# A two-block transformer kernel: attention of the second half before the router, the router on four banks, no filling products

## The chip, the cores and the metric

The kernel runs on one core of a Trainium2 chip. The metric is the device time of one launch in microseconds. A core has TensorE (PE, matrix products), VectorE (DVE), ScalarE (ACT), GpSimd (POOL) and SyncE (SP, which here only issues transfers). Each engine takes its instructions strictly in the order in which they are written; between engines, semaphores tell when a result is there. PSUM, where PE writes, has eight banks of 128 x 512 floats.

## The reference

Eight batches of 128 tokens, 512 wide, go through two blocks:

```
x += tanh(g_xattn[0]) * attention_32_heads(layernorm(x), ctx, rotary, mask)
x += tanh(g_ffn[0])   * (layernorm(x) @ dequantized(W).T + bias)
x += tanh(g_xattn[1]) * softmax(Q K^T / sqrt(512)) @ ctx        # Q from layernorm(x), K from ctx
xf = layernorm(x)                                               # 1024 tokens
logits = xf @ gate_w.T                                          # 32 experts
w, idx = top_k(logits, 2); w = softmax(w)
x += tanh(g_ffn[1]) * sum_k w[k] * (xf @ expert_w[idx[k]].T + expert_b[idx[k]])
```

## The kernel before

A "tile" is 128 tokens, one batch. Tiles 0 to 3 are the first half, 4 to 7 the second. The first attention and the feed-forward take up to about 700 us; the change touches what lies between there and the start of the experts.

**The second attention.** PE makes the query and key projections (`project(i)`, 12 products of 128x512 each), ACT moves each out of PSUM (`keep(i)`). `score(n)` makes the scores of half n into bank 4. DVE takes the maximum (`softmax_shift`), ACT the exponentials (`exps(n)`), PE transposes them into bank 5 (`turn_probs(n)`), ACT copies them (`probs_kept(n)`), PE multiplies with the context, one batch after another, on banks 6 and 7 (`attend(n, batches)`), and DVE adds the result to x and takes the statistics of the next norm (`attended(t)`). `attend` of a tile waits until DVE has emptied the same bank two tiles earlier.

**The router.** For each tile: ACT takes the root (`router_std`), DVE the reciprocal and the shift (`normed`), ACT writes the normalized tile (`router_norm`), PE transposes it (`router_turn`), ACT copies the transpose (`router_kept`), PE multiplies it with the gate weights, four products of 128x32 listed as eight (`logits`), DVE finds the two best experts (`choose`), POOL writes the 0/1 rows (`code`), PE counts how many tokens chose each expert before this one (`rank`), DVE picks the place (`find_place`), POOL marks it (`mark_place`), and PE lays the token numbers at their places (`codes`). Transposes and logits of tile t use bank t % 2, so `router_turn(t)` waits for the choice of tile t-2. `count_all` closes it, DVE reads the places (`write_rows`, place_row, line 1372) and POOL gathers the tokens of each expert by indirect transfers (`take(k)`, line 1048), which also need all eight normalized tiles written to memory (`keep_rows`, on SP).

**Filling products.** `fill(n)` on PE makes n products of 96x128 with 128x512 into bank 4 (line 1621). Nobody reads them. There are 58, between the router's steps and 18 behind `count_all`.

**The experts.** 36 slots follow. For slot k PE transposes the gathered tokens (`turn`, one slot ahead) and makes 12 products of 128x512 (`multiply`, lines 133 to 135). ACT and DVE split tokens and weights into an upper and a lower part. SP keeps a ring of nine expert weights of 1 MB each full; entries 2 to 6 are loaded once `score(1)` is done.

The order is written out by hand for every engine. Each engine's list stands at the end of its function.

Of the kernel before, what the change touches and what calls it, by code (L numbers as in the profile page):

```python
# [9 lines left out]
ALU = mybir.AluOpType  # L10
ACT = mybir.ActivationFunctionType
AX = mybir.AxisListType

P = 128
NB = 8
# [3 lines left out]
KC = E // P  # L19
# [21 lines left out]
def program(nc, a, out):  # L41

    root = ExitStack()
    with root:
# [764 lines left out]
        COMB = 2  # L809
        words = sb("words", [P, 2, KC, E], I32)  # L810
# [108 lines left out]

        def bank_of(k):  # L920
            return psum[(6, 7, 4, 2)[k % LANES]][:, :]
# [14 lines left out]
        with nc.Block() as block:  # L936
            @block.sync
            def _(sp):
# [20 lines left out]
                keep_rows(HALVES[0])  # L959
# [3 lines left out]
                keep_rows(HALVES[1])  # L963
# [38 lines left out]
            def _(pool):  # L1002
# [65 lines left out]
                for t in range(NB - 2):  # L1068
                    mark_place(t)
                    code(t + 2)  # L1070
                mark_place(NB - 2)
# [21 lines left out]
            def _(act):  # L1093
# [26 lines left out]
                def router_std(t):  # L1120
                    act.wait_ge(ln_aggr, 3 * NB + t + 1)
                    nc.scalar.activation(spread[:, t:t + 1], meanvar[:, t, 1:2], ACT.Sqrt, bias=eps[:, :]).then_inc(ln_std, 1)

                def router_norm(t):
                    act.wait_ge(ln_var, 6 + t + 1)
                    nc.scalar.activation(last_xn[:, t, :], x[:, t, :], ACT.Identity, scale=rstd[:, t:t + 1], bias=shift[:, t:t + 1]).then_inc(ln_norm, 1)

                def router_kept(t):
                    act.wait_ge(r_turned, t + 1)
                    after(act, r_logits, t - 1)  # L1130
                    nc.scalar.activation(xr[:, t % 2, :, :], psum[t % 2][:, :].rearrange("p (c t) -> p c t", c=KC), ACT.Copy).then_inc(r_kept, 1)
# [70 lines left out]
                router_std(0)  # L1202
                router_std(1)
                router_norm(0)
                keep(15)
                router_std(2)
                router_norm(1)
                router_std(3)
                router_norm(2)
                router_norm(3)  # L1210
# [5 lines left out]
                router_kept(0)  # L1216
                router_kept(1)
                exps(1)
                probs_kept(1)
                router_kept(2)  # L1220
                router_kept(3)
                router_std(4)
                router_std(5)
                router_norm(4)
                router_kept(4)
                router_std(6)
                router_norm(5)
                router_kept(5)
                router_std(7)
                router_norm(6)  # L1230
                router_kept(6)
                router_norm(7)
# [18 lines left out]
            def _(dve):  # L1251
# [65 lines left out]
                def normed(t):  # L1317
                    dve.wait_ge(ln_std, 6 + t + 1)
                    nc.vector.reciprocal(rstd[:, t:t + 1], spread[:, t:t + 1]).then_inc(ln_rstd, 1)
                    dve.wait_ge(ln_rstd, 6 + t + 1)  # L1320
                    nc.vector.scalar_tensor_tensor(shift[:, t:t + 1], meanvar[:, t, 0:1], -1.0, rstd[:, t:t + 1], ALU.mult, ALU.mult).then_inc(ln_var, 1)

                def choose(t):

                    scores = psum[t % 2][:, 0:NX]
# [130 lines left out]
                attended(1)  # L1456
                normed(0)
                attended(2)
                normed(1)
                attended(3)  # L1460
                normed(2)
                normed(3)
                softmax_shift(1)
                choose(0)
                choose(1)
                softmax_scale(1)
                find_place(0)
                attended(4)
                attended(5)
                normed(4)  # L1470
                choose(2)
                attended(6)
                normed(5)
                find_place(1)
                choose(3)
                attended(7)
                normed(6)
                choose(4)
                find_place(2)
                normed(7)  # L1480
                choose(5)
                find_place(3)
                choose(6)
                find_place(4)
                choose(7)
                find_place(5)
                find_place(6)
                find_place(7)
# [38 lines left out]
            def _(pe):  # L1527
# [55 lines left out]
                def router_turn(t):  # L1583
                    pe.wait_ge(ln_norm, 3 * NB + t + 1)
                    if t < 2:
                        pe.wait_ge(ln_lo, 3 * NB)
                    else:
                        pe.wait_ge(r_best, 2 * t - 2)
                    for c in range(KC):
                        mm = nc.tensor.transpose(psum[t % 2][:, c * P:(c + 1) * P], last_xn[:, t, c * P:(c + 1) * P], ident[:, :])  # L1590
                    mm.then_inc(r_turned, 1)

                def logits(t):
                    pe.wait_ge(g_gate, 16)
                    pe.wait_ge(r_kept, t + 1)
                    for c in range(KC):
                        mm = nc.tensor.matmul(psum[t % 2][:, 0:NX], xr[:, t % 2, c, :], gw[:, c, :], start=c == 0, stop=c == KC - 1)  # L1597
                    mm.then_inc(r_logits, 1)
# [18 lines left out]

                def fill(n):

                    for _ in range(n):  # L1620
                        nc.tensor.matmul(psum[4][:, :], ones[0:3 * NX, :], eb3[:, :], start=True, stop=True)  # L1621
# [96 lines left out]
                attend(0, range(4))  # L1718
                project(15)
                score(1)  # L1720
                for t in range(2):
                    router_turn(t)
                    logits(t)
                router_turn(2)
                router_turn(3)
                turn_probs(1)
                rank(0)
                attend(1, range(2))
                logits(2)
                logits(3)  # L1730
                rank(1)
                codes(0)
                attend(1, range(2, 4))
                pe.wait_ge(constants, 2)
                fill(4)
                router_turn(4)
                fill(4)
                logits(4)
                rank(2)
                codes(1)  # L1740
                fill(4)
                router_turn(5)
                fill(4)
                logits(5)
                rank(3)
                codes(2)
                fill(4)
                router_turn(6)
                fill(4)
                logits(6)  # L1750
                rank(4)
                fill(4)
                router_turn(7)
                codes(3)
                fill(4)
                logits(7)
                rank(5)
                codes(4)
                fill(4)
                rank(6)  # L1760
                codes(5)
                fill(2)
                rank(7)
                codes(6)
                fill(2)
                codes(7)
                count_all()
                fill(18)
# [75 lines left out]
```

## Time and profile before

| | us |
|---|---|
| median of 3 timed runs | 932.43 (931.3 to 934.28) |
| the profiled execution's own time | 926.58 |
| its span, first to last instruction | 924.8 |
| PE busy, of the span | 845.8 (91%) |
| DVE busy | 661.4 (72%) |
| ACT busy | 398.5 (43%) |
| mean granted clock of PE | 0.964 |

Times in rows are from the span's start. "Granted clock" is the share of PE's full speed of 2.4 GHz; 0.50 is 1.2 GHz. A busy PE isn't a PE that does needed work: the filling products count as busy.

### The profile page before, as it was taken

The numbers are of one execution on the slowest core, as the hardware profiler recorded it, in microseconds if no ns is written. First come the engines' busy times: TensorE is split into PE (matmuls) and PEld (weight loads), VectorE is DVE, ScalarE is ACT, GpSimd is POOL, SyncE is SP. The second block draws the span as 40 slices with busy tenths as digits, with TensorE's granted clock in tenths as the row PEclk, the third lists the DMA queues.
The fourth block names the chain that finished last, engine by engine and source line by source line (L and its number), as shares of the span: only waits on it lengthen the run. The fifth ranks groups of instructions, "written<-read, shape, count | busy, mean of one in ns | idle before, by whom it ended". The sixth has DMA issues, their size and how long they took to land. (4 is left out here: it accounts for less than half of the span.)

```text
span 924.8 us, 13194 instructions
## 1 busy us (share of the span) xinstructions
PE 845.8 (91%) x4370; PEld 708.1 (77%) x4370; DVE 661.4 (72%) x1311; ACT 398.5 (43%) x1012; POOL 431.2 (47%) x390
## 2 busy tenths in 40 slices
PE   5688999999999999999999999987989898989990
PEld 4676788888888888888888888866877676877870
DVE  4947688876778776788886788775372556999974
ACT  4334334424325433434433433444124545978970
POOL 5449636534626642734833633512020148876730
PEclk9878999999999999999999999999999998999995
DMA  8301301200200300110200120006100645999817
GB/s 330 152 1 46 114 1 35 80 1 2 84 31 0 113 0 0 45 68 1 84 29 0 45 91 1 1 1 245 46 11 1 232 178 193 340 351 337 331 43 274
DMA packets 23641, 91.13 MB, mean 99 GB/s; under 512 B 6576, under 2 KB 7088, under 8 KB 15776
## 3 DMA queue, kind: packets, MB, share of 16 engines
q1 hardware_dynamic: 17440, 81.00, 23.8%
q0 software_dynamic: 6144, 9.46, 2.9%
q8 instruction: 25, 0.41, 0.2%
q14 instruction: 32, 0.26, 0.1%
HBM read 86.23 MB, written 14.68 MB: 109 GB/s over the span
## 5 line engine op out<-in xcount | busy, mean ns | idle before, releaser
L359 POOL TENSOR_TENSOR qT<-straight,turned 128x512 f32<-128x512 f32 x64 | 82.5, 1290 | 154.8 <-DVE turned L557 154.5
L455 ACT ACTIVATE probs<-bank,negmax 128x128 f32<-128x128 f32 x256 | 90.5, 365 | 134.0 <-DVE negmax L568 134.0
L557 DVE TENSOR_TENSOR turned<-bank,sinT 64x512 f32<-64x512 f32 x160 | 110.1, 688 | 2.2
L133 PE MATMUL bank<-wo_hi,oT_hi 128*128 128x512 f32 x256 | 101.5, 397 | 8.2 <-DVE oT_lo L581 6.2
L133 PE MATMUL bank<-xT_hi,wq_hi 128*128 128x512 f32 x256 | 105.3, 411 | 1.0 <-POOL wq_lo L338 1.0
L135 PE MATMUL bank<-xT_hi,wq_lo 128*128 128x512 f32 x256 | 100.9, 394 | 0.0
L134 PE MATMUL bank<-xT_lo,wq_hi 128*128 128x512 f32 x256 | 100.7, 393 | 0.0
L135 PE MATMUL bank<-wo_hi,oT_lo 128*128 128x512 f32 x256 | 100.4, 392 | 0.0
L134 PE MATMUL bank<-wo_lo,oT_hi 128*128 128x512 f32 x256 | 100.3, 392 | 0.0
L462 ACT ACTIVATE pT_hi<-bank 128x512 fp32r<-128x512 f32 x64 | 38.3, 599 | 131.2 <-PE bank L722 131.2
L555 DVE TENSOR_TENSOR straight<-bank,cosT 128x512 f32<-128x512 f32 x80 | 55.2, 691 | 45.4 <-PE bank L135 44.9
L363 POOL TENSOR_TENSOR probs<-probs,invtotal 128x512 f32<-128x512 f32 x64 | 66.7, 1043 | 20.6 <-DVE invtotal L573 20.6
L1443 DVE TENSOR_TENSOR cT_lo<-ring,cT_hi 128x1024 fp32r<-128x1024 f32 x56 | 68.3, 1221 | 11.1 <-ACT cT_hi L1155 11.1
L715 PE MATMUL bank<-kT,qT 128*128 128x128 f32 x512 | 69.9, 281 | 5.8 <-POOL qT L359 5.8
L586 DVE SCALAR_TENSOR_TENSOR x<-bank,gates,x 128x512 f32<-128x512 f32 x64 | 47.9, 748 | 34.7 <-PE bank L135 34.7
L564 DVE COPY_PREDICATED_SCALAR bank<-closed_key,masked 128x128 f32 x256 | 71.1, 346 | 1.9 <-issue 1.8
L467 ACT ACTIVATE oT_hi<-bank 128x512 fp32r<-128x512 f32 x64 | 38.6, 604 | 73.7 <-PE bank L135 73.7
L715 PEld LDWEIGHTS bank<-kT,qT 128*128 128x128 f32 x512 | 63.9, 196 | 6.7 <-issue 4.6
L133 PE MATMUL bank<-cT_hi,xT_hi 128*128 128x512 f32 x144 | 60.5, 420 | 5.8 <-DVE xT_lo L1437 5.8
L133 PEld LDWEIGHTS bank<-wo_hi,oT_hi 128*128 128x128 f32 x256 | 48.3, 189 | 20.6 <-DVE oT_lo L581 7.5
L581 DVE TENSOR_TENSOR oT_lo<-bank,oT_hi 128x512 fp32r<-128x512 f32 x64 | 44.2, 691 | 25.0 <-ACT oT_hi L467 23.6
L1056 POOL DMA_INDIRECT picked<-loaded,place_row x36 | 44.2, 1227 | 33.6 <-ACT loaded L1161 25.2
(226 smaller groups left out, 2121.5 us busy)
## 6 DMA issues: line engine op xcount, KB each, us to landing
ring<-in_ew SPq DMA_DIRECT2D x28, 1024.0 KB, 8.3
raw_big<-in_wq SPq DMA_DIRECT2D x8, 1024.0 KB, 4.8
raw_big<-in_wo SPq DMA_DIRECT2D x8, 1024.0 KB, 4.8
early_w<-in_ew SPq DMA_DIRECT2D x8, 1024.0 KB, 8.0
ring<-picked SPq DMA_DIRECT2D x8, 512.0 KB, 6.9
raw_k<-in_wk SPq DMA_DIRECT2D x8, 256.0 KB, 5.0
ctx_raw<-in_ctxT SPq DMA_DIRECT2D x4, 512.0 KB, 6.1
raw_v<-in_wv SPq DMA_DIRECT2D x8, 256.0 KB, 5.0
```

Of the source, the lines that this page charges most:

```text
L133: nc.tensor.matmul(out_, hi, r_hi, start=start, stop=False)
L134: nc.tensor.matmul(out_, hi, r_lo, start=False, stop=False)
L135: return nc.tensor.matmul(out_, lo, r_hi, start=False, stop=stop)
L359: nc.gpsimd.tensor_tensor(dst, straight[:, k, :], turned[:, k, :], ALU.add).then_inc(rope_sum, 1)
L363: nc.gpsimd.tensor_tensor(probs[:, u % 2, :, :], probs[:, u % 2, :, :], invtotal[:, u % UNITS, :].unsqueeze(2).broadcast_to([P, GR, S]), A ...
L455: ex = nc.scalar.activation(probs[:, u % 2, h, :], bank_scores[u % 2][:, h * S:(h + 1) * S], ACT.Exp, bias=negmax[:, u % UNITS, h:h + 1], ...
L555: nc.vector.tensor_tensor(straight[:, k, :], bank[:, :], cosT[:, tok], ALU.mult)
L557: last = nc.vector.tensor_tensor(turned[dst, k, :], bank[src, :], sinT[src, tok], ALU.mult)
L564: kept_ = nc.vector.copy_predicated(bank_scores[u % 2][:, h * S:(h + 1) * S], closed_key[:, u, :], masked[:, :].broadcast_to([P, S]))
L586: nc.vector.scalar_tensor_tensor(x[:, u % UNITS, :], bank_y[:, :], gates[:, 0:1], x[:, u % UNITS, :], ALU.mult, ALU.add).then_inc(y_added, 1)
L715: mm = nc.tensor.matmul(bank_scores[u % 2][:, h * S:(h + 1) * S], qT[:, u // 4, h, q], kT[:, keys], start=True, stop=True)
L1443: nc.vector.tensor_tensor(expert_lo(k)[:, rows, :], ring[k % RING][:, rows, :], expert_hi(k)[:, rows, :].bitcast(F32), ALU.subtract).then_ ...
```

## The change

1. PE: `project(15)` stands ahead of the attention of the first half, `score(1)` behind two of its batches. The second half's probabilities and all four of its batches come before any router step. Then the router runs with nothing else between its steps.
2. All `fill` calls are gone.
3. The router has four banks, 0, 1, 4 and 5: `router_turn(t)` waits for the choice of tile t-4.
4. Root, reciprocal and shift are made for tiles 0-3, 4-5 and 6-7 together (`NORMED`), in 3 instructions of each kind for 8.
5. ACT: the exponentials of the second half come before the first root. DVE's order follows PE's.
6. SP: loads of ring entries 2 to 6 stand ahead of all writes of normalized tiles.
7. The marks of tiles 5, 6 and 7 are made by DVE, where only that of tile 7 was; POOL marks tiles 0 to 4.

```diff
+        MARKED = 5
+        NORMED = ((0, 4), (4, 6), (6, 8))
+        def router_bank(t):
+            return psum[(0, 1, 4, 5)[t % 4]]
...
-                keep_rows(HALVES[0])
                 sp.wait_ge(g_smm, 2)
                 for k in range(EARLY, RING - 2):
                     sp.dma_start(ring[k], a["ew"][k]).then_inc(w_in[k], 16)
-                keep_rows(HALVES[1])
+                keep_rows(TILES)
...
-                def router_std(t):
-                    act.wait_ge(ln_aggr, 3 * NB + t + 1)
-                    nc.scalar.activation(spread[:, t:t + 1], meanvar[:, t, 1:2], ACT.Sqrt, bias=eps[:, :]).then_inc(ln_std, 1)
+                def router_std(g):
+                    first, last = NORMED[g]
+                    act.wait_ge(ln_aggr, 3 * NB + last)
+                    nc.scalar.activation(spread[:, first:last], meanvar[:, first:last, 1], ACT.Sqrt, bias=eps[:, :]).then_inc(ln_std, 1)
...
-                    if t == NB - 1:
+                    if t >= MARKED:
                         dve.wait_ge(r_place, 2 * t + 2)
-                        dve.wait_ge(r_at, NB - 1)
+                        dve.wait_ge(r_at, t)
...
                 def router_turn(t):
                     pe.wait_ge(ln_norm, 3 * NB + t + 1)
-                    if t < 2:
+                    if t < 4:
                         pe.wait_ge(ln_lo, 3 * NB)
+                        pe.wait_ge(g_pkept, 2)
                     else:
-                        pe.wait_ge(r_best, 2 * t - 2)
+                        pe.wait_ge(r_best, 2 * t - 6)
...
+                for t in range(2, NB):
                     logits(t)
+                    if t + 2 < NB:
+                        router_turn(t + 2)
+                    rank(t - 1)
+                    codes(t - 2)
+                pe.wait_ge(g_added, NB)
...
-                fill(18)
                 turn(0)
```

PE's queue before, from the first half's attention to the router's fifth tile. `gw` are logits, `ident,words` transposes of router tiles, `l1_ctx` attention, `l1_k` scores, `eb3` filling products; the 12 products of a projection are left out.

```order
L1581 MATMUL bank7<-l1_ctx,l1_pT 128x512
...
L1563 MATMUL bank4<-l1_k,weight 128x128 x16
L1590 MATMUL bank0<-ident,words 128x128 x4
L1597 MATMUL bank0<-gw,x_router_4171 128x32 x4
...
L1581 MATMUL bank7<-l1_ctx,l1_pT 128x512
L1621 MATMUL bank4<-eb3_4190,ones_4168 128x512 x4
L1590 MATMUL bank0<-ident,words 128x128 x4
L1621 MATMUL bank4<-eb3_4190,ones_4168 128x512 x4
L1597 MATMUL bank0<-gw,x_router_4171 128x32 x4
L1607 MATMUL bank2<-chosen_4166,ones_4168 128x224
```

The same place in the changed kernel, with the same names (`l1_probs` is the transpose of the probabilities):

```order
L1570 MATMUL bank7<-l1_ctx,l1_pT 128x512
L1552 MATMUL bank4<-l1_k,weight 128x128 x16
L1570 MATMUL bank6<-l1_ctx,l1_pT 128x512
L1570 MATMUL bank7<-l1_ctx,l1_pT 128x512
L1560 MATMUL bank5<-ident,l1_probs 128x128 x4
...
L1570 MATMUL bank7<-l1_ctx,l1_pT 128x512
L1580 MATMUL bank0<-ident,words 128x128 x4
L1580 MATMUL bank1<-ident,words 128x128 x4
L1587 MATMUL bank0<-gw,x_router_4171 128x32 x4
L1580 MATMUL bank4<-ident,words 128x128 x4
```

The scores now come between two pairs of batches, and the first router transpose comes behind the last batch instead of behind the scores. Farther on, the changed queue repeats this for each tile, with nothing between (here the logits of tile 4, the transpose of tile 6, the count of tile 3 and the codes of tile 2):

```order
L1587 MATMUL bank0<-gw,x_router_4171 128x32 x4
L1580 MATMUL bank4<-ident,words 128x128 x4
L1597 MATMUL bank2<-chosen_4166,ones_4168 128x192
L1600 MATMUL bank2<-chosen_4166,before_4167 128x32
L1612 MATMUL bank3<-onehot_code_4169,xT_lo 128x32 x2
```

Before, eight filling products (line 1621) stood among these rows for every tile.

## Rows read from the trace of the kernel before

**Rows 1.** Busy time by stretch: PE, weight loads, DVE, ACT, POOL, clock, DMA share, GB/s.

```profile
727.60:768.18 40.58, 36.89 (x200) 29.95 (x198) 22.44 (x96) 16.43 (x31) 17.49 (x36) 0.87 0.59 220
768.18:925.00 156.82, 124.51 (x609) 100.69 (x607) 127.85 (x159) 107.70 (x150) 90.53 (x75) 0.92 0.76 274
```

**Rows 2.** Chain of waits, attention to first experts: start, us, what.

```profile
715.73 0.88 PE bank L1581 x2
...
723.80 3.84 PE bank L1563 x32
...
732.20 1.77 PE bank L1590 x8
...
746.71 0.93 PE bank L1621 x4
747.64 0.90 PE bank L1597 x8
748.97 1.01 PE bank L1621 x4
749.98 0.44 PE bank L1590 x4
...
770.95 4.11 DMA words<-xn_rows,place_token
775.11 0.66 PE bank L1656 x4
```

**Rows 3.** Busy time by stretches of 2 us, columns as in rows 1.

```profile
728.00:730.00 2.00, 1.22 (x12) 1.18 (x12) 0.61 (x3) 0.60 (x1) 0.56 (x1) 1.00 1.02 304
732.00:734.00 2.00, 2.00 (x11) 1.52 (x11) 0.84 (x5) 1.81 (x9) 0.50 (x2) 0.53 0.98 410
736.00:738.00 2.00, 2.00 (x10) 1.07 (x8) 1.12 (x2) 1.89 (x3) 0.92 (x2) 1.00 0.98 414
758.00:760.00 2.00, 1.08 (x6) 0.90 (x6) 0.44 (x2) 0.00 (x0) 1.97 (x5) 0.86 0.67 279
760.00:762.00 2.00, 1.97 (x8) 1.78 (x8) 0.55 (x3) 1.15 (x2) 0.00 (x0) 0.50 0.04 12
766.00:768.00 2.00, 2.00 (x10) 1.65 (x9) 1.44 (x3) 0.00 (x0) 1.84 (x3) 0.94 0.19 51
776.00:778.00 2.00, 2.00 (x7) 1.56 (x7) 1.38 (x3) 1.34 (x2) 1.59 (x2) 0.62 0.97 387
```

**Rows 4.** Costliest group of 714 to 768 us: busy, mean ns, idle before.

```profile
L1621 PE MATMUL bank<-eb,ones 96*128 96x512 f32 x58 | 19.1, 465 | 0.0
```

**Rows 5.** Timeline, instructions in order of time: start, us, engine, line [idle before].

```profile
727.67 2.77 SPq L962 DMA_DIRECT2D ring<-in_ew  x5
727.68 0.69 DVE L1295 TENSOR_REDUCE l_max<-bank 128x4 f32<-128x512 f32 x1 [2.47 <-PE bank L1563]
...
731.03 1.28 ACT L1112 ACT_TABLE_LOAD   x1
732.32 0.37 ACT L1112 ACTIVATE l_probs<-bank,l_nb 128x128 f32<-128x128 f32 x1
...
733.88 1.11 PE L1571 MATMUL bank<-ident,l_probs 128*128 128x128 f32 x4
...
742.38 0.60 PE L1590 MATMUL bank<-ident,words 128*128 128x128 f32 x4
...
743.02 0.60 ACT L1131 ACTIVATE x_router<-bank 128x512 f32<-128x512 f32 x1 [1.81 <-PE bank L1590]
...
743.70 0.80 ACT L1126 ACTIVATE words<-x,shift,rstd 128x512 f32<-128x512 f32 x1
...
743.76 1.05 PE L1597 MATMUL bank<-gw,x_router 128*128 128x32 f32 x8
...
761.96 0.19 DVE L1372 TENSOR_SCALAR place_row<-bank 128x32 int32<-128x32 f32 x1 [1.37 <-PE bank L1627]
761.97 6.37 PE L1621 MATMUL bank<-eb,ones 96*128 96x512 f32 x18
```

More of the change, by code:

```diff
@@ L1067, in _ @@
                 code(1)
-                for t in range(NB - 2):
+                for t in range(MARKED):
                     mark_place(t)
                     code(t + 2)
-                mark_place(NB - 2)
+                code(MARKED + 2)
                 pool.wait_ge(rows_out, 16 * NB)
@@ L1130, in router_kept @@
                     after(act, r_logits, t - 1)
-                    nc.scalar.activation(xr[:, t % 2, :, :], psum[t % 2][:, :].rearrange("p (c t) -> p c t", c=KC), ACT.Copy).then_inc(r_kept, 1)
+                    nc.scalar.activation(xr[:, t % 2, :, :], router_bank(t)[:, :].rearrange("p (c t) -> p c t", c=KC), ACT.Copy).then_inc(r_kept, 1)
                 def weight_exp():
@@ L1201, in _ @@
                 keep(14)
-                router_std(0)
-                router_std(1)
-                router_norm(0)
                 keep(15)
[L1206 to L1210, printed above, removed]
                 act.wait_ge(m_const, 64)
@@ L1215, in _ @@
                 nc.scalar.activation(eb3[:, :], eb_raw[:, :], ACT.Copy).then_inc(exact, 1)
-                router_kept(0)
-                router_kept(1)
                 exps(1)
                 probs_kept(1)
+                router_std(0)
+                router_norm(0)
+                router_norm(1)
+                router_kept(0)
+                router_std(1)
+                router_norm(2)
+                router_kept(1)
+                router_norm(3)
                 router_kept(2)
+                router_norm(4)
                 router_kept(3)
-                router_std(4)
-                router_std(5)
-                router_norm(4)
+                router_std(2)
+                router_norm(5)
                 router_kept(4)
-                router_std(6)
-                router_norm(5)
+                router_norm(6)
                 router_kept(5)
-                router_std(7)
-                router_norm(6)
+                router_norm(7)
                 router_kept(6)
-                router_norm(7)
                 router_kept(7)
@@ L1315, in attended, with normed @@
                     nc.vector.bn_aggr(meanvar[:, t, :], stats[:, t, :]).then_inc(ln_aggr, 1)
[L1317 to L1321, printed above, removed]
+                def normed(g):
+                    tiles = slice(*NORMED[g])
+                    dve.wait_ge(ln_std, 6 + g + 1)
+                    nc.vector.reciprocal(rstd[:, tiles], spread[:, tiles]).then_inc(ln_rstd, 1)
+                    dve.wait_ge(ln_rstd, 6 + g + 1)
+                    nc.vector.scalar_tensor_tensor(shift[:, tiles], meanvar[:, tiles, 0], -1.0, rstd[:, tiles], ALU.mult, ALU.mult).then_inc(ln_var, 1)
                 def choose(t):
-                    scores = psum[t % 2][:, 0:NX]
+                    scores = router_bank(t)[:, 0:NX]
                     dve.wait_ge(r_logits, t + 1)
@@ L1456, in _ @@
                 attended(1)
+                softmax_shift(1)
+                attended(2)
+                attended(3)
+                softmax_scale(1)
+                attended(4)
                 normed(0)
-                attended(2)
+                attended(5)
+                attended(6)
+                choose(0)
                 normed(1)
-                attended(3)
+                choose(1)
+                find_place(0)
+                attended(7)
+                choose(2)
                 normed(2)
[L1462 to L1473, printed above, removed]
-                find_place(1)
[L1475 to L1488, printed above, removed]
+                find_place(1)
+                for t in range(3, NB):
+                    choose(t)
+                    find_place(t - 1)
+                find_place(NB - 1)
                 weight_diff()
@@ L1596, in logits @@
                     for c in range(KC):
-                        mm = nc.tensor.matmul(psum[t % 2][:, 0:NX], xr[:, t % 2, c, :], gw[:, c, :], start=c == 0, stop=c == KC - 1)
+                        mm = nc.tensor.matmul(router_bank(t)[:, 0:NX], xr[:, t % 2, c, :], gw[:, c, :], start=c == 0, stop=c == KC - 1)
                     mm.then_inc(r_logits, 1)
@@ L1616, in count_all @@
                                      start=False, stop=True, skip_group_check=True).then_inc(r_rank, 1)
-                def fill(n):
-                    for _ in range(n):
-                        nc.tensor.matmul(psum[4][:, :], ones[0:3 * NX, :], eb3[:, :], start=True, stop=True)
                 def codes(t):
@@ L1717, in _ @@
                 project(14)
-                attend(0, range(4))
                 project(15)
+                attend(0, range(2))
                 score(1)
-                for t in range(2):
-                    router_turn(t)
-                    logits(t)
[L1724 to L1766, printed above, removed]
+                attend(0, range(2, 4))
+                turn_probs(1)
+                attend(1, range(4))
+                router_turn(0)
+                router_turn(1)
+                logits(0)
+                router_turn(2)
+                logits(1)
+                rank(0)
+                router_turn(3)
+                for t in range(2, NB):
+                    logits(t)
+                    if t + 2 < NB:
[3 more added lines that the diff above has]
+                pe.wait_ge(g_added, NB)
+                rank(NB - 1)
+                codes(NB - 2)
+                codes(NB - 1)
                 count_all()
-                fill(18)
                 turn(0)
```

4 lines of the change are left out of this document (2 added, 2 removed).

## The prediction

> **What bounds the kernel now.** I read the busy time by stretches first [rows 1]. The change begins near 715 us and ends where the experts start, so what lies before it, and the 157 us behind it, stay as they are unless something is handed on to them. In the stretch from 727.60 to 768.18 PE is busy 36.89 of 40.58 us, but 58 filling products make up the costliest group there, 19.1 us of listed busy time [rows 1, 4]. Their ends overlap; a group of four takes 0.93 us of the chain of waits [rows 2], so 0.23 us each. That is the second thing to see: in the steady part of the router the chain of waits runs through PE alone, filling products 0.93, logits 0.90, then 0.43 for count and codes (748.97 less 748.54), filling products 1.01, transposes 0.44, so that they lie on the path and aren't in its gaps [rows 2]. Third, the clock. After the stretch from 728 on, in which PE was busy 1.22 of 2 us, it was 0.53 in 732 to 734; it was back at 1.00 in 736 to 738; and after 758 to 760, busy 1.08 of 2 us, it was 0.50 in 760 to 762 and 0.94 in 766 to 768 [rows 3]. The filled part between ran at full clock. So the filling products cost time and buy clock, and the whole case turns on the balance.
>
> The end of the stage is the instruction on DVE that reads the places, place_row, at 761.96 [rows 5]. Everything behind it (gathers, combining weights, experts) keeps its distance to it unless PE's clock changes there. I count in that instruction's time.
>
> **The head of the stage.** Before, the first half's attention (715.73) and then the last projection came ahead of the second half's scores at 723.80 [rows 2]. Attention takes 0.88 us a batch on PE [rows 2], about 0.92 with its wait. Now the projection goes first: 12 products of 0.23 us are 2.78, from 715.57 to 718.35; two batches bring 720.19, and the projection's copy on ACT is ready before. The scores start at 720.2 for 723.8, 3.6 us earlier, and take 3.7 us, to 723.9. What comes next was far apart before: the maximum on DVE began 3.88 us after the scores (727.68 for 723.80), but the exponentials only at 732.32, behind router copies and a table load of 1.28 us on ACT [rows 5]. Now the exponentials are next on ACT and its table is still that of the first half. By the rows: maximum at 724.1, exponentials some 0.9 us later at 725.0 (the maximum's 0.69 and a small scaling), transpose of the probabilities 1.5 later (733.88 for 732.32 [rows 5]) at 726.5, copy 0.64 later and attention 0.74 after that, as between transposes, copy and logits of a router tile (742.38, 743.02, 743.76 [rows 5]), at 727.8. PE has the two other batches of the first half meanwhile. Four batches of 0.92 would take 3.7 us; DVE, which adds and takes the statistics of each tile and must have emptied the bank, holds them to 4.8, so they end at 732.6. The first router transpose stands there; the first norm, behind one table load and one root, is ready at 731.7 and costs nothing. Before, that transpose was at 727.6, but tiles 4 to 7 waited until 742.38 [rows 5]; now all eight follow at once.
>
> The Trainium skill, "ScalarE: Activation LUTs", section on what a table load costs, gives about 2.66 us a switch, load and drain. Here the load began at 731.03 and the exponential at 732.32: 1.29 us, nothing beside it [rows 5], and the measurement decides. Of five such loads in this stage the change leaves three; none of the two that go is a term of its own, they are part of the wait for the exponentials above.
>
> **The router at full clock.** From rows: transposes 0.44 us of PE, logits startable 1.38 us after the transposes began (743.76 for 742.38), logits 0.90, count and codes 0.43 [rows 2, 5]. PE so needs 1.77 us a tile, 1.83 with waits. ACT needs 0.60 + 0.80 = 1.4 a tile [rows 5]. DVE and POOL are busy 22.44 and 17.49 us of the stretch with all else that they do there [rows 1], and POOL gives two tiles' marks away. With four banks, the 1.38 us and the choice behind the logits fit into three other tiles' work. I walked the four queues of the changed kernel with these durations: 8 tiles of PE work are 14.6 us, the first copy adds 0.5, tile 5's norm 0.1, the first codes behind POOL's mark 0.6, and the last tile's choice, count, place, mark and codes, with nothing left beside them, some 3. 732.6 + 19 gives place_row at 752.05: 9.9 us earlier. This is the best that the change can bring.
>
> **The router at half clock.** Eight transposes took 1.77 us in the chain at clock 0.53 [rows 2, 3], 0.89 a tile and twice the 0.44. No row shows the 128x32 products alone at half clock; their bounds are 0.89 (no change) and 1.8 (they double like the transposes). I take 1.8: transposes are the nearest row, the same weight load and product for each. Then a tile needs 0.89 + 1.8 + 0.75 = 3.45 us of PE. With half clock from the first router transpose on, the walk gives 761.7, a gain of 0.3. With 1.3 for the logits it gives 757.7, a gain of 4.2.
>
> **Which clock.** The changed router is the same transposes and logits as before 732, with hardly a gap: busier than the 1.22 of 2 us after which the clock fell, but without the filling products beside which it held. The four attention batches ahead of it (732.6) are as dense as those at 736 to 738 at which it stood at 1.00 [rows 3]. So I expect full clock over the first two or three tiles and half for most of the rest. With the fall at 739 the walk gives 757.7 (5 logits 9.0, 3 transposes 2.7, the counts and codes left 5, the tail 2), a gain of 4.2; with a fall at 735.5, 759.1 and 2.9; with the clock going up and down between 735.5 and 752, 755 to 756 and 6 to 7. I take 4.2.
>
> The Trainium skill, "TensorE: Matmul & The Clock Gate", section on a second failure mode, says that small idle gaps between groups of products are enough to let the clock go up and down. The trace agrees at 732 and 760 [rows 3]; by that rule full clock throughout is unlikely, and 752.05 isn't my forecast.
>
> **Behind the router.** The 18 filling products behind count_all run from 761.97 and end at 768.3 [rows 5], and the first expert transposes wait for them. Gone, slot 0 can start when its gather has landed. It gains nothing: slot 1 waits for the gather issued at 770.95 behind the combining weights, and its transposes start at 775.11, 13.15 us behind place_row [rows 2]. But they also warmed PE for slot 0. Cold, its 12 products take up to twice 2.8 us, from about 8.5 us behind place_row to 14, against the 13.15 at which slot 1 may begin. Slot 1 is hit by half clock before as well: 0.62 in 776 to 778 [rows 3], which I put at 2 us. I put this part at 0. Its good end is those 2 us saved; its bad end is two more slots at half clock, 5.6, and 0.9 of a late start, less the 2 already paid: 4.5 lost.
>
> **SP.** Five loads of 1 MB, issued at 727.67 before [rows 5], now go at 724.1, and all eight writes of normalized tiles stand behind them. At the 410 GB/s of the rows [rows 3] they take 12.8 us, to 737. The first normalized tile is ready at 731.7 and waits in the queue, the last at 742 to 747 doesn't. The gather needs them all, 5 us later at least. The last two ring loads follow at about 745, and before that they followed at 752; both are done before the gather. The cost is 0, unless place_row came before 749. Three roots for eight, and the two further marks on DVE, hide beside PE.
>
> **The sum.** 926.58, the profiled execution's own time, less 4.2 is 922.4. That execution lies 5.85 us below the median of the timed runs. Carried over, 932.43 - 4.2 = 928.2, and the following times are all of this kind.
>
> **The rivals.**
> - Full clock holds through the router: for it speaks that PE then has hardly a gap; against it, what fell at 732 was made of the same transposes and logits. Gain 9.9 less up to 1.5 of cold first slots: 922.5 to 924.
> - Half clock from the first tile: for it, the same fall at 732; against it, the four dense batches. Gain 0.3: 932.1, no change.
> - Slower: half clock from the first tile, and it lasts through expert slots 0, 1 and 2, since the 18 products that brought it back at 766 are gone [rows 3]. That is the bad end above, 4.5 lost against 0.3 gained: 936.6. It decides once less than 4 us are gained in the router. Against it, the dense half-clock work at 776 to 778 didn't keep it down: the experts' whole stretch has 0.92 [rows 1, 3].
> - The reordering doesn't bring the scores forward, because something of the first half (DVE's additions, which now come beside them) is late. DVE had been idle 2.47 us when the maximum came [rows 5]; worth 1 us at most, and inside the range.
>
> **How the numbers follow.** The forecast, a gain of 2.8 to 7, has 0.40; full clock 0.17; no change 0.26; slower 0.17. About 0.3%, 2.8 us, is what a measurement can tell from no change. Faster is 0.40 + 0.17 = 0.57, same 0.26, slower 0.17. The forecast's own range is 925.4 to 929.6. Holding eight of ten cuts the far end of both sides: 922.8 to 935.
>
> **What would show it.** Scores at 720 and the first router transpose near 732.6; logits of neighbouring tiles 1.8 us apart at full clock and 3.4 at half; the clock near 1.00 up to 736 to 739 and below 0.7 on average after; place_row near 757.7; slot 1's transposes 13 us behind it. The forecast is wrong if the clock stays at 1.00 to the end of the router, or if logits at half clock take much less than 1.8, or if expert slots 1 and 2 run at half clock.

## The result and the profile after

The changed kernel is faster. In the runs that compare the two, before took 931.07 us (median of 13, 926.65 to 936.2) and after 925.33 us (median of 13, 923.04 to 926.79): a ratio of 0.9937, 95% interval 0.9922 to 0.9952, or 5.7 us less. The forecast was 928.2 us, 4.2 less, with a range of 922.8 to 935. Of all runs of this document one, of 950.12 us (after_allfill, clock 0.942, the other nine 924.5 to 933.4), is a slow run and is left out of its ratio.

The two profiled executions stand closer together than the medians: 926.11 us after (span 924.2, clock 0.955) for 926.58 before (924.8, clock 0.964). Where the other 5 us are is a question of its own, taken up with the experiments.

The page of after, busy time of two engines over the span and its count of instructions:

```profile
span 924.2 us, 13062 instructions
PE 836.8 (91%) x4312; PEld 701.1 (76%) x4312; DVE 661.2 (72%) x1303; ACT 394.8 (43%) x1005; POOL 424.8 (46%) x386
```

The head of the stage, from the timeline of after (start, us, engine, line, idle before in brackets), which answers to [rows 5]:

```profile
721.55 3.73 PE L1552 MATMUL bank<-l_k,weight 128*128 128x128 f32 x32
725.32 0.69 DVE L1295 TENSOR_REDUCE l_max<-bank 128x4 f32<-128x512 f32 x1 [1.05 <-PE bank L1552]
...
726.25 0.37 ACT L1116 ACTIVATE l_probs<-bank,l_nb 128x128 f32<-128x128 f32 x1 [4.62 <-DVE l_nb L1297]
...
727.81 0.65 PE L1560 MATMUL bank<-ident,l_probs 128*128 128x128 f32 x4 [0.81 <-ACT l_probs L1116]
...
734.02 1.04 PE L1580 MATMUL bank<-ident,words 128*128 128x128 f32 x8
735.40 1.05 PE L1587 MATMUL bank<-gw,x_router 128*128 128x32 f32 x8 [0.34 <-ACT x_router L1136]
```

This execution reached the stage 1.48 us later than that of before did: the first half's probabilities are transposed at 713.83 instead of 712.35. So I count from that instruction. From there, in us, before and then after: scores 11.45, 7.72; second half's probabilities 21.53, 13.98; first router transpose 15.13, 20.19; place_row 49.61, 43.18. The exponentials follow the maximum by 0.93 us instead of 4.64.

The router, in stretches of 2 us (busy time and count of PE, weight loads, DVE, ACT, POOL; clock; DMA share; GB/s), which answers to [rows 3]:

```profile
740.00:742.00 2.00, 1.47 (x13) 1.47 (x14) 1.83 (x11) 1.35 (x3) 0.98 (x3) 1.00 0.96 371
742.00:744.00 2.00, 1.17 (x12) 1.07 (x11) 0.94 (x6) 2.00 (x4) 1.91 (x5) 1.00 1.06 408
744.00:746.00 2.00, 2.00 (x15) 2.00 (x14) 0.97 (x6) 0.57 (x2) 1.39 (x4) 0.66 1.16 358
746.00:748.00 2.00, 2.00 (x11) 2.00 (x11) 0.32 (x2) 0.04 (x1) 1.19 (x3) 0.50 0.78 263
...
768.00:770.00 2.00, 1.28 (x5) 0.71 (x3) 0.00 (x0) 0.69 (x2) 1.70 (x2) 0.87 0.52 94
770.00:772.00 2.00, 0.00 (x0) 0.00 (x0) 1.11 (x1) 0.85 (x1) 1.39 (x3) 0.98 0.98 416
772.00:774.00 2.00, 0.53 (x3) 0.53 (x4) 0.11 (x1) 0.00 (x0) 1.70 (x2) 0.50 0.73 265
...
778.00:780.00 2.00, 2.00 (x12) 1.63 (x11) 0.00 (x0) 0.62 (x2) 1.36 (x2) 0.81 0.79 212
```

Full clock up to 744; in the two stretches before the fall PE was busy 1.47 and 1.17 of 2 us. Then half to 768, up for two stretches, and half again to 778. In the same router, the timeline shows the logits at both levels:

```profile
738.39 0.98 PE L1587 MATMUL bank<-gw,x_router 128*128 128x32 f32 x8
...
745.91 1.89 PE L1587 MATMUL bank<-gw,x_router 128*128 128x32 f32 x8
...
749.22 1.89 PE L1587 MATMUL bank<-gw,x_router 128*128 128x32 f32 x8
...
751.78 1.47 PE L1587 MATMUL bank<-gw,x_router 128*128 128x32 f32 x6
```

Eight 128x32 products take 1.89 us at half clock for 0.98 at full clock (the third tile's; other tiles' took up to 1.05). Tiles 5 and 6, between which the transposes of tile 7 stand, are 3.31 us apart (749.22 less 745.91).

Behind the router, the chain of waits of after, which answers to the end of [rows 2]:

```profile
757.01 0.20 DVE place_row L1373
...
761.43 2.02 POOL onehot_w L1035
763.45 0.07 issue
763.51 0.74 POOL comb L1038
764.25 0.06 issue
764.31 1.74 POOL comb L1041 x2
...
767.01 6.42 DMA words<-xn_rows,place_token
773.43 0.04 issue
773.47 1.11 PE bank L1641 x4
```

The gather for slot 1 is issued 10.00 us behind place_row and lands after 6.42 us; before it was issued 8.99 behind and took 4.11 [rows 2]. So slot 1's transposes come 16.46 us behind place_row, for 13.15. Here the change gives back 3.3 us. ("Slot 1's transposes" are the third group of four: they stand ahead of slot 1's products and turn the tokens of slot 2, `turn` being one slot ahead. So they wait for the third gather, `take(2)`.)

### The profile page after: what moved, and what is told of

Read it like the earlier page. It is cut to its first block and busy times, and to the rows that moved or that the text cites. A ratio compares the mean times of both kernels' runs of the same rounds, so it can differ in the third digit from the quotient of the medians.

```text
span 924.2 us, 13062 instructions
## 1 busy us (share of the span) xinstructions
PE 836.8 (91%) x4312; PEld 701.1 (76%) x4312; DVE 661.2 (72%) x1303; ACT 394.8 (43%) x1005; POOL 424.8 (46%) x386
## 5 line engine op out<-in xcount | busy, mean ns | idle before, releaser
L1060 POOL DMA_INDIRECT picked<-loaded,place_row x36 | 41.2, 1146 | 41.3 <-ACT loaded L1166 26.9
```

## The experiments

Each ratio is to the kernel before, on the same chip, with its 95% interval. "Slot 1 at" is the start of slot 1's transposes behind place_row, and place_row is counted from the first half's probabilities, as above.

**after_again, before_again, before_third: how far executions differ.** No edit.

> The changed kernel once more, unaltered, for a second trace of it and for a comparison on the same chip as the three others. Theory A (the gain lies between the first half's attention and place_row, some 6.4 us measured from a common point before it, and part is given back at the second gather and in expert slot 1): place_row again 6 to 7 us nearer to the last instructions of the first half's probabilities than in the kernel before, clock below full from about the fourth router tile, median 5 to 7 us below before. Theory B (the gain of the medians comes from something that varies between executions of the kernel before): ratio anywhere from 0.990 to 1.000, place_row not in the same place within 1 us.

> The kernel before once more, unaltered, for a second trace: the first one's time, 926.58 us, lies at the lower end of its runs (926.65 to 936.2). If the work between the first half's probabilities and the last expert slot varies: place_row not at 49.6 us behind the first transpose of the first half's probabilities, or expert slot 1 not 13.15 us behind place_row. If it doesn't: the same numbers within 0.3 us, and the rest of the difference before 712 us or behind 900 us.

> The same once more, for a third trace, with the same question: which stretch of the kernel before differs between executions by up to 9 us.

After_again: 927.52 us, 0.9938 [0.9917, 0.9960], the same gain a second time; place_row at 43.24, slot 1 at 16.47. The two more of before, one run each: 930.97 and 928.89 us; place_row at 51.48 and 49.61, slot 1 at 12.45 and 13.05. So place_row of before is 49.6 to 51.5, slot 1 12.5 to 13.2, while the two executions of after agree within 0.1: both differences are the change's, not the execution's. The 1.9 us by which before_again is later come with the clock. Two of its stretches:

```profile
736.00:738.00 2.00, 2.00 (x3) 0.89 (x3) 0.17 (x1) 1.92 (x3) 0.96 (x2) 0.50 1.02 430
...
776.00:778.00 2.00, 1.69 (x10) 1.48 (x11) 0.53 (x2) 1.97 (x4) 1.70 (x2) 1.00 0.46 88
```

At 736 it was still at half clock, where before was back at 1.00 [rows 3]. At 776 it is the other way round, 1.00 for 0.62 [rows 3], and slot 2 follows slot 1 by 3.24 us in before_again, by 4.83 in before and 4.82 in before_third.

The 63 runs of before in the comparisons of these experiments say the rest. Those with a clock below 0.9575 (11) have a median of 934.77 us, those from 0.9575 to 0.9625 (32) 932.68, those above (20) 930.64. All three profiled executions of before had 0.964 or 0.965, at the upper end, and their own times, 926.58, 930.97 and 928.89 us, are 928.8 in the mean, where the median of the 63 is 932.35. Those of after had 0.951 and 0.955, at the lower end of its 21 runs (0.951 to 0.960). One profiled pair therefore shows less of the gain than is there.

**before_nofill: the removal without the order.** In the kernel before, all 58 filling products go, and nothing else changes:

```
-                fill(4)
...
-                fill(2)
...
-                fill(18)
```

> The kernel before with all 58 filling products taken out and nothing else changed. Theory A (the new order is what pays; without filling products the clock falls, and in the old order, where each tile's transposes, copy and logits follow one another with nothing between, half clock is not covered): a tile of the router takes about 4.4 us at half clock for 3.67 before, so 0 to 4 us slower than before. Rival (the filling products were the cost, the order does little): 4 to 8 us faster than before, about as fast as the changed kernel.

934.22 us, 1.0024 [1.0004, 1.0044]. place_row comes at 52.03, 1.8 later than the mean of the three executions of before (50.23), and slot 1 at 16.33. The expectation, 0 to 4 us slower, came true: taking the filling products out of the old order is a small loss. It is the order, and the banks that let it run (the next run), that pay.

**after_2banks: the new order on the old two banks.**

```
-            return psum[(0, 1, 4, 5)[t % 4]]
+            return psum[t % 2]
-                    if t < 4:
+                    if t < 2:
-                        pe.wait_ge(r_best, 2 * t - 6)
+                        pe.wait_ge(r_best, 2 * t - 2)
```

> The changed kernel with the router on banks 0 and 1 as before. Theory A (four banks let PE run on; with two each transpose waits for the choice of the tile two back): PE idle 0.6 to 0.7 us a tile for six tiles, place_row 3 to 5 us later than 43.2 behind the first half's probabilities, 3 to 5 us slower than the changed kernel. Rival (at half clock PE's work covers the choice): place_row within 1 us.

932.75 us, 1.0005 [0.9993, 1.0018]: nothing is left of the gain. place_row moves from 43.18 to 49.96, 6.8 us for the 3 to 5 expected. The stretches of 2 us show why:

```profile
738.00:740.00 2.00, 1.41 (x14) 1.35 (x13) 0.89 (x6) 1.30 (x2) 0.45 (x3) 1.00 0.92 266
740.00:742.00 2.00, 1.10 (x11) 0.99 (x9) 1.90 (x7) 0.80 (x3) 1.56 (x4) 0.86 0.91 331
742.00:744.00 2.00, 1.71 (x9) 1.74 (x9) 1.00 (x6) 1.38 (x4) 0.50 (x2) 0.50 1.04 388
744.00:746.00 2.00, 1.78 (x9) 1.64 (x8) 0.32 (x2) 0.71 (x2) 1.18 (x2) 0.50 0.65 251
```

PE has holes from tile 2 on (1.41 and 1.10 of 2 us), the clock falls 3 us sooner than in after (0.86 already in 740 to 742), and at half clock there are still holes. So four banks act in two ways: they take the wait for the choice out of PE's way, and they keep the full clock longer. How the 6.8 us divide between the two isn't shown. The Trainium skill, "TensorE: Matmul & The Clock Gate", section on a second failure mode, ties a clock that goes up and down to small gaps as PE cycles through its banks. The trace agrees that gaps of this kind come before the fall; it fell once and stayed.

**after_fill4 and after_allfill: is the clock worth filling for?** after_fill4 puts back 24 products, two behind each logits and two behind each codes of tiles 2 to 7; after_allfill puts back what before had, four and four a tile and 18 behind count_all.

```
+                    fill(2)        (after_fill4; after_allfill: fill(4))
                     if t + 2 < NB:
                         router_turn(t + 2)
                     codes(t - 2)
+                    fill(2)        (after_allfill: fill(4), and fill(18) at the end)
```

> The changed kernel with two filling products behind each tile's logits and two behind its codes, into bank 6, from the third tile on (24 in all). If the clock is worth more than it costs: full clock to the end of the router, a tile 1.83 + 0.92 = 2.75 us for 3.3 at half clock, place_row about 2 us earlier for the tiles after the fall, but later for the tiles that had full clock anyway; in sum -2 to +2 us against the changed kernel. Rival (any filling product lies on the path and the clock falls all the same): 24 times 0.23 to 0.43 us, 5 to 10 us slower than the changed kernel.

> The changed order with filling products dosed as in the kernel before: four behind the logits and four behind the codes of each of tiles 2 to 7, 18 behind count_all (66 for 58). It parts the order from the filling products. Theory A (products on the path cost about what full clock gives): place_row near 48.5 us behind the first half's probabilities for 43.2, slot 1's transposes back at 13.1 us behind it; 1 to 2 us faster than before at best. Rival (the order is the gain, the products are free): place_row at 43 to 45, 6 us faster than before.

after_fill4: 925.52 us, 0.9924 [0.9898, 0.9951]; place_row at 42.01, 1.2 earlier than in after. The clock stays up to 756:

```profile
744.00:746.00 2.00, 2.00 (x17) 1.92 (x16) 0.50 (x4) 0.60 (x1) 1.57 (x4) 1.00 1.04 255
...
752.00:754.00 2.00, 1.37 (x9) 1.05 (x7) 1.49 (x7) 0.43 (x2) 0.27 (x2) 1.00 0.00 0
...
756.00:758.00 2.00, 0.00 (x0) 0.00 (x0) 1.75 (x12) 0.00 (x0) 1.67 (x3) 0.55 0.21 67
```

So 24 products, at 0.23 us each [rows 2] about 5.5 us of PE, buy back a little more than they cost in the router. The intervals of the two ratios, 0.9924 and 0.9937, overlap, so in time the gain isn't shown. after_allfill: 929.45 us, 0.9950 [0.9927, 0.9973]; place_row at 47.27: full clock to the end of the router, but 4.1 us later than with none. In place_row the dose decides, and no filling is near the best; in time this one, too, isn't told from after. Of its expectation place_row came true in the main (48.5), slot 1 did not: 16.41 for 13.1, though all 18 trailing products are back. More on that below.

**before_no18, after_tail10, after_take4, after_hold10: why slot 1 comes later.** My theory after the first profiles: without the 18 trailing products slot 0 runs sooner, and then two things run into the third gather. The rival: a PE at half clock, since those products also kept it busy.

before_no18 takes `fill(18)` alone out of before; after_tail10 puts ten products behind count_all:

```
                 count_all()
+                pe.wait_ge(constants, 2)
+                fill(10)
                 turn(0)
```

> The kernel before without the 18 filling products behind count_all only. Theory A (they delay expert slot 0, and so the ring load that collides with the third gather): place_row unchanged at 49.6 to 51.5 us, slot 1's transposes at 16.4 us behind it for 13.15, 2 to 3.5 us slower than before. Rival (they only cost): slot 0 earlier, 1 to 2 us faster.

> The changed kernel with ten filling products behind count_all only, into bank 6, in the 4.6 us in which PE waits there for the first gather. Theory A (part of the router's gain is given back by half clock in expert slots 0 and 1): the products at half clock fill the gap, the clock is back at 1.00 in slot 0 or at the start of slot 1, slot 1 takes 3.5 to 4.8 us for 5.7, so 1 to 2 us faster than the changed kernel. Rival (slot 1 is bound by its gather and DVE alone): no difference.

before_no18: 934.33 us, 1.0012 [0.9995, 1.0028], slot 1 at 16.45. In the old order too, the removal of the 18 alone costs 3.3 to 4 us at slot 1. In time it is about 1 us, less than the 2 to 3.5 expected, and not told from none. after_tail10: 926.93 us, 0.9950 [0.9931, 0.9970], slot 1 at 16.39 and slot 2 5.75 us after it; ten products change neither, as the rival had it. They ran from the end of the router and were over when PE had to wait for the gather, in which the clock fell as before (1.00 in 770 to 772, 0.62 and 0.50 in the two stretches after). Filling at this place doesn't bring the clock back for slot 1. Nor is it the clock that makes slot 1 start late: PE had been idle for 4.13 us when the gather landed.

after_take4 issues the gathers of slots 2 and 3 (`take(2)` is the third gather, which slot 1's transposes wait for) ahead of the combining weights; after_hold10 leaves them and keeps back one 1 MB weight load until that gather has landed:

```
 after_take4                                after_hold10, in SP's weights(k)
                 take(1)                    +   if k == RING + 1:
+                take(2)                    +       sp.wait_ge(t_in[2], 16)
+                take(3)
                 combine_weights()
-                for k in range(2, TAKEN):
+                for k in range(4, TAKEN):
```

> The changed kernel with the gathers of expert slots 2 and 3 issued by GpSimd ahead of the combining weights, so the third gather goes 4 us behind place_row for 10, and the combining weights come 2.6 us later. Theory A (slot 1 waits for the third gather alone, which in the changed kernel lands 16.4 us behind place_row): slot 1's transposes about 12.8 us behind place_row, when slot 0 ends, 3 to 3.6 us faster than the changed kernel. Rival (half clock and DVE bound the first slots): slot 1 at 12.8 too, but slot 2 where it was, under 1 us gained.

> The changed kernel with the second ring load behind the router (expert weights 10, 1 MB) held until the third gather has landed; before, that load happened to be issued 2.5 us behind that gather, in the changed kernel it is issued 1 us behind it. Theory A (the gather's 6.4 us for 4.1 are that load's doing): landing after 4 to 4.5 us, slot 1's transposes 14 to 14.5 us behind place_row for 16.4, 1.5 to 2.3 us faster than the changed kernel. Rival (the gather shares with the load issued before, number 9): no difference.

after_take4: 924.18 us, 0.9901 [0.9864, 0.9938]; the gather is issued 4.13 us behind place_row and slot 1 comes at 12.18. after_hold10: 925.70 us, 0.9923 [0.9899, 0.9948]; slot 1 at 14.22. In the traces both did what theory A says; in time both intervals overlap that of after, so the 3.4 and 1.3 us that the ratios give aren't shown.

They also bear on where the half clock in slot 1 comes from. In after it is this stretch:

```profile
776.00:778.00 2.00, 2.00 (x6) 1.52 (x5) 1.22 (x1) 0.17 (x1) 1.70 (x2) 0.50 0.26 60
```

In after PE is idle 4.20 us before slot 1, and slot 2 follows slot 1 by 5.71 us. In after_take4 it isn't idle there, the clock is 1.00 from 770 on, and slot 2 follows by 3.22 us. Without the 18 products but in the old order (before_nofill, before_no18) it is 4.82 and 4.86, as in before. So the missing products aren't what makes slot 1 slow; the half clock there goes with the wait for the gather.

Three lines of after_hold10's chain, to be laid beside those of after:

```profile
766.71 1.78 POOL comb L1043 x2
...
769.45 4.12 DMA words<-xn_rows,place_token
773.58 0.04 issue
773.62 0.66 PE bank L1643 x4
```

The gather takes 4.12 us again, and only the cast's 1.78 is left. When SP issues the two loads, first of after, then of before, then of after_allfill (line, engine, count, duration ns, first and last start):

```profile
L978 SPq DMA_DIRECT2D early_w<-in_ew x2: 327/327/327, 762.6 to 768.0; - x2
```

```profile
L974 SPq DMA_DIRECT2D early_w<-in_ew x2: 327/328/328, 767.5 to 773.6; - x2
```

```profile
L978 SPq DMA_DIRECT2D early_w<-in_ew x2: 327/328/328, 767.3 to 772.6; - x2
```

The second load was issued 2.65 us behind the gather in before (773.6 for 770.95), and 1.0 us behind it in after (768.0 for 767.01). SP issues it when DVE has split the weights of slot 1, work that stands behind slot 0's tokens on DVE. In after_allfill it was 1.0 too (772.6 for 771.63), and the gather took 6.46 us: slot 0 stood at 5.72 behind place_row there, 0.5 sooner than in before, the load 0.8 sooner, and the gather itself 0.9 later. So it isn't the missing products as such; less than 1 us on either side decides how close the load comes to the gather. The other part is the gather's own delay, by the combining weights on POOL. The timeline of before, and then that of after with the durations of its two casts (ns, shortest, median, longest):

```profile
769.25 0.74 POOL L1037 CAST comb<-comb 128x256 fp32r<-128x256 f32 x2
...
770.39 1.50 DVE L1443 TENSOR_TENSOR cT_lo<-early_w,cT_hi 128x1024 fp32r<-128x1024 f32 x1 [0.26 <-ACT cT_hi L1155]
```

```profile
764.52 1.26 DVE L1444 TENSOR_TENSOR cT_lo<-early_w,cT_hi 128x1024 fp32r<-128x1024 f32 x1 [0.26 <-ACT cT_hi L1160]
```

```profile
L1041 POOL CAST comb<-comb x2: 396/892/1387, 764.3 to 764.7; 128x256 fp32r<-128x256 f32 x2
```

In before both casts are over when DVE's subtraction begins. In after the first takes 396 ns; the subtraction starts at 764.52, the second cast at 764.7, and it is done at 766.1, 0.3 us after the subtraction's end at 765.78: it ended only after the subtraction had. Before_nofill (1.73 us) and after_hold10 (1.78) have casts and subtraction side by side as well. In after_allfill the casts are first, and the next instruction on POOL meets the subtraction (at 769.65) instead:

```profile
769.02 0.74 POOL L1041 CAST comb<-comb 128x256 fp32r<-128x256 f32 x2
769.85 1.64 POOL L1044 TENSOR_TENSOR comb<-comb,comb 128x256 fp32r<-128x256 f32 x1
```

That one took 0.74 us in after. The Trainium skill, "SBUF — State Buffer", section on who interferes with whom, states the rule: a DVE instruction with two inputs in SBUF (here early_w and cT_hi) contends with a GpSimd instruction that reads SBUF, for ports that one of the two holds at a time. The traces agree, with the 1387 ns for 396 and the 1.64 us for 0.74. No experiment moved the subtraction alone, so it stays a reading of five profiles.

**after_combo: both finds together.** The edits of after_fill4 and after_take4.

> Meant as a better version: the changed kernel with the gathers of slots 2 and 3 ahead of the combining weights and four filling products a tile from the third tile on. Theory A: the two gains add, 1.2 us in the router and 3 in the first slots, 3 to 4.5 us faster than the changed kernel, ratio to before 0.988 to 0.990. Rival (the filling products' gain is lost again in a slot 0 at half clock): no better than the gathers alone, 0.9901.

922.36 us (921.04 to 924.58), 0.9880 [0.9863, 0.9897]; place_row at 42.23, slot 1 at 12.60. It beats before by 1.2%, and its interval lies below that of after, though it rests on four runs.

The change has more parts than these runs take apart: the roots for several tiles at once, the order on SP and the marks on DVE were not tried by themselves.

## Why the prediction was right, and which steps were not

The gain from place_row is the first term; what is lost behind it is measured from place_row to the transposes of the last slot (before, mean of three: 50.23 and 132.66). The sum of both differences, and what the ratio makes of 931 us (sums are rounded last):

```
                place_row   last slot   sum     timed
after            -7.1        +3.2       -3.8    -5.9
after_again      -7.0        +3.4       -3.6    -5.8
before_nofill    +1.8        +2.0       +3.8    +2.2
before_no18      +1.4        +2.2       +3.6    +1.1
after_fill4      -8.2        +4.5       -3.7    -7.1
after_tail10     -7.1        +3.3       -3.7    -4.7
after_take4      -7.1        +0.3       -6.8    -9.2
after_hold10     -7.0        +0.6       -6.4    -7.2
after_2banks     -0.3        +3.3       +3.1    +0.5
after_allfill    -3.0        +3.0        0.0    -4.7
after_combo      -8.0        +0.4       -7.6    -11.2
```

In each row the time is better than the sum, by 0.8 to 4.7 us, 2.4 in the mean. A surplus that all eleven share most likely belongs to what they are compared with: the profiled executions of before are its good ones. By the clock they stand about 1.7 us below the median (930.64 for 932.35). That is an inference, not a test. The rest, under 1 us in the mean, stays open; so does why identical work ahead of the change ends anywhere from 711.9 to 716.1.

**The head** was right to 0.1 us: scores 3.73 earlier for 3.6, router transposes at 20.19 for 20.25. The four batches beside DVE's additions took 5.04 us (729.15 to 734.19 in the chain of waits) for 4.8.

**The clock** did what the forecast's case says: full over the first tiles, then half. It fell behind 744 (743 on the clock of before, whose stage began 1.48 us sooner) and not at 739, after five tiles' logits and not two or three. That is the term mis-sized: place_row came 6.4 us sooner by the profiled pair, 7.0 against the mean of before, for the 4.2. Two tiles' logits less at half clock, 0.9 us each, are most of the difference. The "clock going up and down" case had 6 to 7, but nothing went up and down in the router.

**Logits at half clock**, the choice between 0.89 and 1.8: 1.89, so the nearest row was right. Neighbouring tiles 3.3 us apart for the 3.4 named.

**The removal**, treated in the prediction as what sets the balance, is worth 4.1 us of place_row in the new order, against the old dose; against 24 products it loses 1.2. In time neither shows beyond the intervals.

**Behind the router** was the wrong step: "It gains nothing: slot 1 waits for the gather issued at 770.95 behind the combining weights, and its transposes start at 775.11, 13.15 us behind place_row". I took the distance of that gather to place_row as fixed. It isn't: its issue sits behind the combining weights on POOL, and its transfer beside a load that SP issues when DVE has split slot 1's weights. Both moved against it: 1.0 and 2.3 us. Slot 0 did run at half clock, as the prediction feared, but its products ended 12 us behind place_row, before the gather landed, so that cost nothing here. The half clock that I priced is there in slot 1: slot 2 follows slot 1 by 5.71 us for 4.83 before, 0.9 us, and no further slot is late by it. But it goes with the wait for the gather and not with the missing 18 products.

**The slower rival**, half clock through slots 0 to 2 at 4.5 us, came to about that size (3.2 to 3.4) by another way, and its condition, less than 4 us won in the router, didn't hold. The full-clock rival was wrong from 744 on; it took filling to hold the clock, and that costs its own time. Its place_row, 752.05, isn't what its own terms add up to either: 732.6 and 14.6, 0.5, 0.1, 0.6 and 3 are 751.4. **SP**: the five loads went at 725.3, the last two at 744.4, both over before place_row: 0, as said.

So the forecast of 928.2 lay 2.9 us above 925.33: 1.4 because the median of before was 931.07 in this comparison and not 932.43, and 1.5 of gain. The two errors in the mechanism nearly cancel (2.2 to 2.8 us more won in the router, 3.2 to 3.4 lost behind it), so the closeness of the number is partly luck. What they leave, 3.6 to 3.8 us by the table, is less than the 4.2 forecast; that the measured gain is more is the surplus above.

## What to carry to other kernels

When a wait is taken away, follow not only who is released but what the released work then starts: here a weight load that DVE's work releases came close behind the third gather and, with the combining weights' delay on POOL, took back 3.3 of some 7 us. Two lines that move the gather ahead (take(2) and take(3)) had slot 1 back at its old place, or sooner. Not all of such a lead lasts: after_take4 was 6.8 us ahead of after at slot 2's transposes (15.40 for 22.17 behind place_row) and 2.9 ahead at the last slot's. Filling products are a dose, to be tried in small ones, and more banks can do part of what filling does for the clock: with four the router held it up to 744, with two up to 741. Profile a kernel more than once before subtracting two profiles: three executions of before differed by 1.9 us at one and the same instruction.

## What the runs showed of the hardware

- A gather of one tile took 4.1 us with a 1 MB load issued 2.65 us behind it or held back, and 6.2 to 6.5 us when the load was issued 1.0 us behind it (eight profiles). In before_again, where the load went only when it had landed, it took 3.24.
- A pair of 128x256 casts on POOL took 0.74 us ahead of a 128x1024 subtraction on DVE and 1.73 to 1.78 us beside it; the single cast that met it in after took 1387 ns for 396.
- Eight 128x32 products with their weight loads took 0.98 to 1.05 us at full and 1.89 at half clock: they nearly double, narrow as they are.
- Twelve products of a slot with its transposes (slot 1 to slot 2) took 3.2 us at full clock (before_again, after_take4), 4.8 with part of them at half (before) and 5.7 with most of them at half (after).
- The kernel before, untouched, ran anywhere between 927.6 us (mean clock 0.965) and 936.9 (0.954). Its time went with the clock, though not strictly: the run with the highest, 0.969, took 932.2.
